# Second cross attention: where the two closing value groups and the output copy of a head stand among the next head's work

## The chip, the cores and the metric

The program runs on one core of one Trainium2 chip. Its engines are TensorE (PE in the profile, PEld for its weight loads), VectorE (DVE), ScalarE (ACT), GpSimd (POOL) and SyncE (SP). The metric is the device time of one execution in microseconds; the time of a kernel is the median over its runs.

## The reference, cut to what matters

The model is a chain of blocks on 256 latent rows of width 256. The block in question is the second cross attention: 16 heads of width 16, 256 queries against 4096 keys.

```python
def _L1_xattn_ref(query, key, value, mask, Wq, bq, Wk, bk, Wv, bv, Wo, bo):
    q = _split_heads(query @ Wq.T + bq)
    k = _split_heads(key @ Wk.T + bk)
    v = _split_heads(value @ Wv.T + bv)
    scores = jnp.einsum('bhqd,bhkd->bhqk', q, k) / jnp.sqrt(jnp.float32(DK))
    scores = jnp.where(mask, scores, jnp.float32(-1000000000.0))
    p = jax.nn.softmax(scores, axis=-1)
    out = jnp.einsum('bhqk,bhkd->bhqd', p, v)
    out = out.transpose(0, 2, 1, 3).reshape(query.shape[0], -1, D)
    return out @ Wo.T + bo
```

The blocks before it (a first cross attention, a self attention, a ternary feed-forward) and behind it (a causal self attention, a mixture of experts) are not touched by the change.

## The kernel before, in words

`stage_cross1` (L1357) holds the block. Every engine has its own instruction stream there, written out by hand; streams meet only at semaphores. The order inside a stream is the order of the text, and nothing plans it.

The 16 heads are walked in pairs (`pairs_of_heads`, L1382): head pair 0 is written out, pairs 1 to 6 are a hardware loop, pair 7 is written out. `b` is the head's place in its pair and picks one of two buffers. One head `h` has these pieces:

- `qk(it, b, g)` (L1568), g = 0 to 7: four TensorE matmuls that write the scores of 512 keys, transposed, into two PSUM banks. Even g use banks 0 and 1, odd g banks 2 and 3. Group 0 waits for `m_rows` of its head, groups wait for the exponential two groups earlier.
- the exponential of group g (L1486) on ScalarE: one ACTIVATE from the two banks into `probs`.
- `pv(h, b, g)` (L1589): the value matmuls of group g, four column blocks of 32, in two passes each (8 matmul records); they add up in PSUM bank 4 over all eight groups. Group 0 waits for `v_staged` and for `acc_copied` of the head before, because it overwrites bank 4.
- `copy_acc(h, b)` (L1500) on ScalarE: copies bank 4 to `acc_sb`, once all eight value groups of head h are done; it raises `acc_copied`.
- `sel(h, b)` (L1600): four small matmuls that read `acc_sb`; VectorE then divides (`normalise`, L1710).
- `m_scores` (L1531): the row maxima of a head are found ahead of time. Sixteen matmuls of 512 keys each per head, taken one head early, rotate over PSUM banks 5 to 7; each is read by one VectorE reduction (L1704), and the bank's next user waits for that read. `m_some(n0, n1)` (L1643) issues the n0-th to (n1-1)-th of them among the current head's work.
- `m_turn` (L1556): two small matmuls at the end of a head that turn the next head's maxima into bank 0; `m_rows` (L1492) on ScalarE then copies them into `q_st`, behind the eighth exponential, and that is what `qk` group 0 of the next head waits for.

TensorE's stream of one head is the `body` at L1637. In short, with the numbers of the groups, before the change:

```text
pv6 pv7 (of the head before) | m0 | qk0 | m1 m2 m3 | qk1 | m4 | qk2 | m5 | pv0 pv1 | m6 | qk3 | m7 m8 m9 | qk4 | m10 |
qk5 | m11 | pv2 pv3 | sel (head before) | m12 | qk6 | m13 | qk7 | m14 m15 | pv4 pv5 | m_turn (next head)
```

Head 0 has no pv6 and pv7 ahead of it and no `sel`. Head 15 has no m's, and head 14 only the first twelve. ScalarE's stream of one head (L1479) is exp0, the copy of the head before, exp1 to exp7, `m_rows` of the next head. POOL stages `v_st` and `q_st` of the next head (L1435), released by the value groups and the scores of the head before the current one; SP loads keys (`load_k1_quarter`, L1348), released by counts of finished score groups (L1416).

Of the kernel before, what the change touches and what calls it, by code (L numbers as in the profile page):

```python
# [1356 lines left out]
def stage_cross1(k):  # L1357
# [18 lines left out]
    def scores_bank(g):  # L1376
        return k.ps[:, 2 * (g % 2):2 * (g % 2) + 2, :].rearrange("p b (c q) -> p (b c) q", q=S)

    def turned(n):
        return k.ps[0:STACK, n, :].bitcast(BF16)  # L1380
# [22 lines left out]
    with nc.Block() as block:  # L1403
# [64 lines left out]
        @block.scalar  # L1468
        def _(act):
            sc = nc.scalar  # L1470
            act.wait_ge(s["q_turned"], 1)
            sc.activation(k.q_st[0:STACK, :, :].rearrange("p b q -> p (b q)"), turned(ACC_BANK)[:, 0:2 * S], ACT.Copy).then_inc(s["q_first"], 1)
            for n in range(H // 4):
                h0 = 2 if n == 0 else 4 * n
                act.wait_ge(s["q_turned"], n + 2)
                sc.activation(k.q_all[0:STACK, h0:4 * n + 4, :].rearrange("p h q -> p (h q)"), turned(n)[:, (h0 - 4 * n) * S:4 * S], ACT.Copy
                              ).then_inc(s["q_stack"], 1)

            def body(it, first, last):  # L1479
                for b in range(2):  # L1480
                    for g in range(groups):
                        n = 16 * it + 8 * b + g
                        act.wait_ge(s["scores"], n + 1)
                        if not (first and b == 0):
                            act.wait_ge(s["pv"], n - groups + 1)
                        sc.activation(probs[:, g], scores_bank(g), ACT.Exp).then_inc(s["exp"], 1)  # L1486
                        if g == 0 and not (first and b == 0):
                            copy_acc(2 * it + b - 1, 1 - b)
                    if not (last and b == 1):
                        m_rows(2 * it + b + 1, 1 - b, first and b == 0)  # L1490

            def m_rows(h, b, fresh=False):  # L1492
                act.wait_ge(s["m_turned"], h + 1)
                if fresh:
                    act.wait_ge(s["q_first"], 1)
                else:
                    act.wait_ge(s["q_staged"], h - 1)
                sc.activation(k.q_st[MAXROW:LOROW, b, :], k.ps[MAXROW:LOROW, 0, 0:S], ACT.Copy).then_inc(s["m_rows"], 1)

            def copy_acc(h, b):  # L1500
                act.wait_ge(s["pv"], groups * h + groups)
                sc.activation(k.acc_sb[:, b, :], k.ps[:, ACC_BANK, 0:S], ACT.Copy).then_inc(s["acc_copied"], 1)

            m_rows(0, 0, True)
            pairs_of_heads(act, body)
            copy_acc(H - 1, 1)

        @block.tensor
        def _(pe):
# [58 lines left out]
            def qk(it, b, g, masked, first):  # L1568
                h, j = 2 * it + b, 2 * b + g // GROUPS
                n = groups * h + g  # L1570
                if g == 0:
                    pe.wait_ge(s["m_rows"], h + 1)
                if g % 2 == 0:
                    pe.wait_ge(k_in[b][g // 2], 16 * K_LOADS1 * (it + 1))
                if not (first and b == 0 and g < 2):
                    pe.wait_ge(s["exp"], n - 1)
                out = scores_bank(g)
                for c in range(GROUP_CH):
                    ch = GROUP_CH * (g % GROUPS) + c
                    last = t.matmul(out[:, c, :], k.k_st[0:STACK, j, ch * P:(ch + 1) * P], k.q_st[0:STACK, b, :],  # L1580
                                    start=True, stop=not masked)
                    if masked:
                        ch = GROUP_CH * g + c
                        for q in range(QT):
                            last = t.matmul(out[:, c, q * P:(q + 1) * P], k.mask_bias[:, q, ch * P:(ch + 1) * P],
                                            k.ident_bf[:, :], start=False, stop=(q == QT - 1))
                last.then_inc(s["scores"], 1)
# [22 lines left out]
            def all_heads(masked):  # L1610
                keep_busy(k, 4, 6, D)
                pe.wait_ge(k.sem("c_aq"), 1)
                o = k.ps[:, 2, :].bitcast(BF16)
                for q in range(QT):
                    for c in range(KT):
                        last = t.transpose(o[:, c * S + q * P:c * S + (q + 1) * P], k.a_q[:, q, c * P:(c + 1) * P], k.ident_bf[:, :])
                last.then_inc(k.sem("c_aqT_ps"), 1)
                pe.wait_ge(k.sem("c_aqT"), 1)
                rows_linear(k, k.a_qT, KT, k.w_tern, None, 3, k.sem("c_y"))
                keep_busy(k, 5, 6)  # L1620
                pe.wait_ge(k.sem("c_xn"), QT)
                transpose_rows(k, k.xn, 2, k.sem("c_xnT_ps"))
                pe.wait_ge(k.sem("c_xnT"), 1)
                rows_linear(k, k.xnT, KT, k.w1_q, None, 3, k.sem("d_q"))
                keep_busy(k, 2, 6)
                pe.wait_ge(s["rows"], 1)
                turn_first()
                for idx in range(n_m):
                    m_scores(0, 0, idx, masked, True, True)
                    if 11 <= idx < 11 + H // 4:  # L1630
                        turn(idx - 11)
                for idx in range(M_AHEAD):
                    m_scores(0, 1, idx, masked, True, True)
                pe.wait_ge(s["q_stack"], H // 4)
                m_turn(0, 0, True)

                def body(it, first, last):  # L1637
                    for b in range(2):
                        h = 2 * it + b
                        behind = not (first and b == 0)  # L1640
                        before = behind and not (first and b == 1)

                        def m_some(n0, n1):  # L1643
                            for x in m_beside(it, b, n0, n1, last):
                                m_scores(*x, masked, first)

                        if behind:
                            pv(h - 1, 1 - b, groups - 2, not before)
                            pv(h - 1, 1 - b, groups - 1, not before)
                        m_some(0, 1)  # L1650
                        qk(it, b, 0, masked, first)
                        m_some(1, 4)
                        qk(it, b, 1, masked, first)
                        m_some(4, 5)
                        qk(it, b, 2, masked, first)
                        m_some(5, 6)
                        pv(h, b, 0, not behind)
                        pv(h, b, 1, not behind)
                        m_some(6, 7)
                        qk(it, b, 3, masked, first)  # L1660
                        m_some(7, 10)
                        qk(it, b, 4, masked, first)
                        m_some(10, 11)
                        qk(it, b, 5, masked, first)
                        m_some(11, 12)
                        pv(h, b, 2, not behind)
                        pv(h, b, 3, not behind)
                        if behind:
                            if last and b == 1:
                                sel(h - 1, 1 - b, n_m * H, H - 2)  # L1670
                            else:
                                sel(h - 1, 1 - b, n_m * (h + 1) + n_m - 2, None)
                        m_some(12, 13)
                        qk(it, b, 6, masked, first)
                        m_some(13, 14)
                        qk(it, b, 7, masked, first)
                        m_some(14, 16)
                        pv(h, b, 4, not behind)
                        pv(h, b, 5, not behind)
                        if not (last and b == 1):  # L1680
                            m_turn(*((it, 1) if b == 0 else (it + 1, 0)))

                pairs_of_heads(pe, body)
                for g in range(groups - 2, groups):
                    pv(H - 1, 1, g, False)
                keep_busy(k, 1, 2, D)
                sel(H - 1, 1, n_m * H, H - 1)
                keep_busy(k, 1, 2, D)

            masked = pe.value_load(k.masked_i[0:1, 0:1], min_val=0, max_val=1)  # L1690
# [503 lines left out]
```

## Time and profile before

| what | value |
|---|---|
| median of 3 runs | 700.41 us (699.09 to 701.73) |
| the profiled execution's own time | 700.59 us |
| its span, first to last instruction | 698.8 us |
| second cross attention, from the first qk to the last copy | about 358.6 to 547.1 us of the span |
| PE, whole span | busy 618.0 us (88%), 5014 matmuls |
| ACT, whole span | busy 453.5 us (65%) |
| DVE, whole span | busy 407.2 us (58%) |

A row of the timeline gives the start in microseconds from the span's start, the time from the first start to the last end of the instructions merged in it, engine, line, operation, output and inputs, shapes, and their number; brackets hold the idle time of that engine before the row and what ended it ("issue" means nothing that the profile shows). Matmuls are pipelined: a matmul's record lasts longer than the step to the next one, so the cost of a piece on TensorE is read from start to start. Times per head are compared from a point of one head to the same point of the next.

### The profile page before, as it was taken

Reading aid. Unit: us, or ns where it says so; the run is one execution under the profiler, and the core shown is the slowest. Engines: PE = TensorE matmul, PEld = TensorE weight load, DVE = VectorE, ACT = ScalarE, POOL = GpSimd, SP = SyncE. Lnnn points to the kernel's source line nnn. Section 1 sums busy time; section 2 is a strip of 40 time slices with the busy share of each in tenths; the row PEclk is TensorE's granted clock in tenths of the full one; section 3 lists DMA queues with packets and bytes.
Section 4 is the critical chain, followed back from the end, with each engine's and each line's share of the span. In section 5 each row is a group of like instructions: output and inputs, shape, how many; then the busy total and the mean of one; then the engine's idle time right before and its main releaser. Section 6 shows DMA issues by size and latency. Waiting matters only on the chain. (4 is left out here: it accounts for less than half of the span.)

```text
span 698.8 us, 14299 instructions
## 1 busy us (share of the span) xinstructions
PE 618.0 (88%) x5014; PEld 374.2 (54%) x5014; DVE 407.2 (58%) x899; ACT 453.5 (65%) x543; POOL 69.1 (10%) x151
## 2 busy tenths in 40 slices
PE   6888887887887888796799999999999998898998
PEld 5554444444344444464345555555554575674886
DVE  6467354222313225876798989898884326645634
ACT  2988999999999993682057767676777215503111
POOL 3001110000010000101211121211110000000000
PEclk8899999999999999998889999999999999999999
DMA  5886786376444113200027633322220570000000
GB/s 132 234 254 206 237 237 211 102 232 173 132 131 127 58 46 118 52 1 3 1 74 248 182 93 81 84 77 86 75 86 10 168 239 1 2 0 1 0 1 15
DMA packets 52904, 73.57 MB, mean 105 GB/s; under 512 B 11044, under 2 KB 29796, under 8 KB 52860
## 3 DMA queue, kind: packets, MB, share of 16 engines
q1 hardware_dynamic: 52091, 72.25, 35.0%
q10 hardware_dynamic: 768, 0.73, 0.4%
q8 instruction: 29, 0.48, 0.3%
q14 instruction: 16, 0.12, 0.1%
HBM read 58.90 MB, written 12.85 MB: 103 GB/s over the span
## 5 line engine op out<-in xcount | busy, mean ns | idle before, releaser
L1704 DVE TENSOR_REDUCE sb_m_blk<-ps 128x1 f32<-128x512 f32 x256 | 159.5, 684 | 18.5 <-PE ps L1550 17.2
L1486 ACT ACTIVATE sb_probs<-ps 128x1024 f32<-128x1024 f32 x128 | 125.8, 1025 | 49.9 <-PE ps L1580 49.3
L656 ACT ACTIVATE sb_probs<-ps 128x1024 f32<-128x1024 f32 x128 | 124.0, 1023 | 10.4 <-PE ps L721 8.9
L661 ACT ACTIVATE sb_probs<-sb_probs,sb_neg_cap,sb_cap 128x4096 f32<-128x4096 f32 (+2 forms) x34 | 121.9, 3591 | 0.1
L740 PE MATMUL ps<-sb_probs,sb_v_st 128*32 128x256 f32 x1024 | 74.5, 388 | 37.2 <-ACT sb_probs L661 37.2
L721 PE MATMUL ps<-sb_q_st,sb_k_st 112*128 112x256 bf16 x512 | 79.3, 280 | 5.2 <-DMA sb_k_st<-k_parts_l 4.4
L1580 PE MATMUL ps<-sb_q_st,sb_k_st 115*128 115x256 bf16 x512 | 76.3, 272 | 1.4 <-ACT sb_probs L1486 1.4
L1550 PE MATMUL ps<-sb_k_st,sb_q_m 96*128 96x512 bf16 x224 | 76.5, 383 | 0.0
L721 PEld LDWEIGHTS ps<-sb_q_st,sb_k_st 112*128 112x128 bf16 x512 | 42.9, 99 | 58.3 <-issue 28.9
L1596 PE MATMUL ps<-sb_probs,sb_v_st 128*32 128x256 f32 x1024 | 67.4, 384 | 0.2 <-ACT sb_probs L1486 0.2
L740 PEld LDWEIGHTS ps<-sb_probs,sb_v_st 128*32 128x32 f32 x1024 | 23.7, 108 | 64.8 <-ACT sb_probs L661 45.5
L1580 PEld LDWEIGHTS ps<-sb_q_st,sb_k_st 115*128 115x128 bf16 x512 | 48.7, 97 | 18.0 <-issue 1.4
L1596 PEld LDWEIGHTS ps<-sb_probs,sb_v_st 128*32 128x32 f32 x1024 | 31.2, 109 | 27.3 <-issue 14.3
L1149 ACT ACTIVATE sb_q_all<-ps,sb_nmax 128x256 f32<-128x256 f32 (+1 forms) x72 | 31.7, 452 | 12.1 <-DVE sb_nmax L1165 12.1
L1018 PE MATMUL ps<-sb_w_o,sb_ones_sq 128*128 128x512 f32 (+1 forms) x82 | 35.0, 564 | 4.8 <-issue 4.8
L1550 PEld LDWEIGHTS ps<-sb_k_st,sb_q_m 96*128 96x128 bf16 x224 | 22.7, 101 | 30.0 <-DVE sb_m_blk L1704 17.1
L617 POOL TENSOR_TENSOR sb_v_st<-sb_v_rows,sb_keep 128x512 f32<-128x512 f32 x14 | 15.9, 1133 | 200.9 <-PE ps L740 161.1
L921 DVE COPY sb_acc_sb<-ps 128x256 f32<-128x256 f32 x16 | 6.8, 424 | 42.3 <-PE ps L740 42.3
L927 DVE RECIPROCAL sb_rec<-ps 128x2 f32<-128x2 f32 x16 | 2.7, 170 | 48.9 <-PE ps L748 48.9
L1165 DVE TENSOR_REDUCE sb_nmax<-ps 128x2 f32<-128x512 f32 (+1 forms) x36 | 22.6, 632 | 13.3 <-PE ps L1088 7.0
L1140 ACT ACTIVATE sb_q_all<-ps 128x512 f32<-128x512 f32 (+1 forms) x36 | 19.8, 551 | 15.6 <-PE ps L1101 15.4
L2008 ACT ACTIVATE sb_probs<-ps 128x512 f32<-128x512 f32 x9 | 5.4, 597 | 36.9 <-PE ps L1966 36.9
(284 smaller groups left out, 846.6 us busy)
## 6 DMA issues: line engine op xcount, KB each, us to landing
sb_k_st<-k_parts_l SPq DMA_DIRECT2D x223, 64.0 KB, 2.0
sb_k_st<-k_parts_l SPq DMA_DIRECT2D x93, 128.0 KB, 3.2
k_parts_l<-sb_v_proj SPq DMA_DIRECT2D x24, 256.0 KB
k_parts_l<-sb_early SPq DMA_DIRECT2D x48, 128.0 KB
sb_v_proj<-ctxT_blocks SPq DMA_DIRECT2D x8, 512.0 KB, 7.0
sb_v_rows<-ctx_by_pair SPq DMA_DIRECT2D x7, 512.0 KB, 4.2
sb_early<-ctxT SPq DMA_DIRECT2D x6, 512.0 KB, 3.8
sb_k_st<-k_parts_l SPq DMA_DIRECT2D x64, 32.0 KB, 1.8
```

The costliest lines, as they stand in the source:

```text
L656: a.activation(probs[:, slot, 4 * g:4 * g + 4, :], scores_bank(g), ACT.Tanh).then_inc(s["tanh"], 1)
L661: a.activation(part, part, ACT.Exp, bias=k.neg_cap[:, 0:1], scale=k.cap[:, 0:1]).then_inc(s["exp"], 1)
L721: last = t.matmul(out[:, c, :], k.k_st[0:STACK0, j, n * P:(n + 1) * P], k.q_st[0:STACK0, j // 2, :], start=True, stop=True)
L740: last = t.matmul(k.ps[32 * m:32 * m + 32, 4 + b, 0:S], k.v_st[:, b, (j % 2) * UNIT_CH + ch, :], probs[:, j % 2, ch, :], start=(j % 2 == 0 ...
L1018: k.nc.tensor.matmul(k.ps[:, bank, 0:cols], k.ones_sq[:, :], k.w1_o[:, :, :].rearrange("p t n -> p (t n)")[:, 0:cols], start=True, stop=True)
L1149: sc.activation(k.sp_rows[:, n % 2, e, 0:nk], a.scores(n)[:, e, 0:nk], ACT.Exp, bias=k.nmax[:, 2 * n + e:2 * n + e + 1], accum_out=k.sums[ ...
L1165: v.tensor_reduce(k.nmax[:, 2 * n:2 * n + 2], a.scores(n)[:, :, 0:nk], AX.X, ALU.max, negate=True).then_inc(s["max"], 1)
L1486: sc.activation(probs[:, g], scores_bank(g), ACT.Exp).then_inc(s["exp"], 1)
L1550: last = t.matmul(o, qs[0:MAXROW, b, q * P:(q + 1) * P], k.k_st[0:MAXROW, 2 * b + blk // (m_blocks // 2), key0:key0 + 512], start=True, st ...
L1580: last = t.matmul(out[:, c, :], k.k_st[0:STACK, j, ch * P:(ch + 1) * P], k.q_st[0:STACK, b, :], start=True, stop=not masked)
L1596: last = t.matmul(k.ps[32 * m:32 * m + 32, ACC_BANK, 0:S], k.v_st[:, b, GROUP_CH * g + m, :], probs[:, g, m, :], start=(g == 0), stop=(g = ...
L1704: v.tensor_reduce(k.m_blk[:, b, q, blk:blk + 1], k.ps[:, m_bank(m_turn_of(idx)), :], AX.X, ALU.max).then_inc(s["m_read"], 1)
```

## The change

On TensorE, the last two value groups of the head before (pv6, pv7) move from the front of a head to behind its score group 0; two of the m matmuls stand ahead of that group and one behind it. On ScalarE, the copy of the head before moves from behind exp0 to behind exp1. No instruction is added or taken away.

```diff
@@ ScalarE, body @@
                         sc.activation(probs[:, g], scores_bank(g), ACT.Exp).then_inc(s["exp"], 1)
-                        if g == 0 and not (first and b == 0):
+                        if g == 1 and not (first and b == 0):
                             copy_acc(2 * it + b - 1, 1 - b)
@@ TensorE, body @@
+                        m_some(0, 2)
+                        qk(it, b, 0, masked, first)
+                        m_some(2, 3)
                         if behind:
                             pv(h - 1, 1 - b, groups - 2, not before)
                             pv(h - 1, 1 - b, groups - 1, not before)
-                        m_some(0, 1)
-                        qk(it, b, 0, masked, first)
-                        m_some(1, 4)
+                        m_some(3, 4)
                         qk(it, b, 1, masked, first)
                         m_some(4, 5)
                         qk(it, b, 2, masked, first)
```

## Rows read from the trace of the kernel before

**Rows 1.** Busy time by engine; columns: stretch, length, PE, PEld, DVE, ACT, POOL, clock, DMA.

```profile
417.62:429.53 11.91, 11.91 (x119) 6.80 (x118) 10.45 (x19) 8.41 (x10) 1.81 (x6) 1.00 0.32 82
...
100.00:111.90 11.90, 10.38 (x101) 6.24 (x94) 5.56 (x9) 11.75 (x10) 1.40 (x2) 1.00 0.66 218
```

**Rows 2.** Waits from 370 to 524.8 us: who, released by, total us, times, longest.

```profile
ACT sb_probs L1486 <- PE ps L1580: 41.6, 48, 1.3
...
PEld ps L1596 <- ACT sb_probs L1486: 2.5, 12, 0.2
```

**Rows 3.** Timeline of PE, the start of one head up to behind its first value groups.

```profile
417.62 0.39 PE L1550 MATMUL ps<-sb_k_st,sb_q_m 96*128 96x512 bf16 x1
417.85 0.60 PE L1580 MATMUL ps<-sb_q_st,sb_k_st 115*128 115x256 bf16 x4
418.29 0.90 PE L1550 MATMUL ps<-sb_k_st,sb_q_m 96*128 96x512 bf16 x3
419.03 0.60 PE L1580 MATMUL ps<-sb_q_st,sb_k_st 115*128 115x256 bf16 x4
...
420.12 0.38 PE L1550 MATMUL ps<-sb_k_st,sb_q_m 96*128 96x512 bf16 x1
420.43 1.07 PE L1596 MATMUL ps<-sb_probs,sb_v_st 128*32 128x256 f32 x16
421.44 0.39 PE L1550 MATMUL ps<-sb_k_st,sb_q_m 96*128 96x512 bf16 x1
```

**Rows 4.** Timeline of PE across the boundary to the next head.

```profile
427.56 1.28 PE L1596 MATMUL ps<-sb_probs,sb_v_st 128*32 128x256 f32 x19
428.46 0.28 PE L1564 MATMUL ps<-sb_ident_bf,sb_m_parts 128*3 128x128 bf16 x2
428.58 1.03 PE L1596 MATMUL ps<-sb_probs,sb_v_st 128*32 128x256 f32 x13
429.54 0.39 PE L1550 MATMUL ps<-sb_k_st,sb_q_m 96*128 96x512 bf16 x1
```

**Rows 5.** Timeline of ACT in the same head and across the same boundary.

```profile
418.49 1.02 ACT L1486 ACTIVATE sb_probs<-ps 128x1024 f32<-128x1024 f32 x1 [1.25 <-PE ps L1580]
419.41 0.38 ACT L1502 ACTIVATE sb_acc_sb<-ps 128x256 f32<-128x256 f32 x1
419.67 1.95 ACT L1486 ACTIVATE sb_probs<-ps 128x1024 f32<-128x1024 f32 x2
...
428.86 0.38 ACT L1498 ACTIVATE sb_q_st<-ps 3x256 bf16<-3x256 f32 x1 [0.34 <-PE ps L1564]
```

**Rows 6.** Timeline of DVE, the last four maxima reads ahead of that boundary.

```profile
426.38 2.48 DVE L1704 TENSOR_REDUCE sb_m_blk<-ps 128x1 f32<-128x512 f32 x4
```

**Rows 7.** Timeline of PEld, the weight loads in the head of rows 3.

```profile
418.18 0.21 PEld L1550 LDWEIGHTS ps<-sb_k_st,sb_q_m 96*128 96x128 bf16 x2
418.80 0.10 PEld L1550 LDWEIGHTS ps<-sb_k_st,sb_q_m 96*128 96x128 bf16 x1 [0.41 <-DVE sb_m_blk L1704]
...
420.43 0.16 PEld L1596 LDWEIGHTS ps<-sb_probs,sb_v_st 128*32 128x32 f32 x8 [0.29 <-issue]
...
421.43 0.10 PEld L1550 LDWEIGHTS ps<-sb_k_st,sb_q_m 96*128 96x128 bf16 x1 [0.41 <-DVE sb_m_blk L1704]
```

**Rows 8.** Timeline of PE in the last head, which has no maxima.

```profile
537.99 0.60 PE L1580 MATMUL ps<-sb_q_st,sb_k_st 115*128 115x256 bf16 x4 [0.77 <-ACT sb_probs L1486]
538.51 1.21 PE L1596 MATMUL ps<-sb_probs,sb_v_st 128*32 128x256 f32 x16
539.65 1.05 PE L1580 MATMUL ps<-sb_q_st,sb_k_st 115*128 115x256 bf16 x8
...
546.02 0.64 PE L1596 MATMUL ps<-sb_probs,sb_v_st 128*32 128x256 f32 x8 [0.16 <-ACT sb_probs L1486]
```

**Rows 9.** Timeline of ACT in the last head.

```profile
535.57 0.38 ACT L1498 ACTIVATE sb_q_st<-ps 3x256 bf16<-3x256 f32 x1
536.82 1.02 ACT L1486 ACTIVATE sb_probs<-ps 128x1024 f32<-128x1024 f32 x1 [0.87 <-PE ps L1580]
...
544.03 1.94 ACT L1486 ACTIVATE sb_probs<-ps 128x1024 f32<-128x1024 f32 x2 [0.87 <-PE ps L1580]
```

## The prediction, made before the result was known

> **What bounds the kernel now.** I read the busy times of stretches first. In one whole head of the second cross attention, 11.91 us long, TensorE's records cover all 11.91 us, VectorE's 10.45 and ScalarE's 8.41 [rows 1]. So the stage runs at TensorE's pace, with VectorE not far behind and ScalarE with room. The table of waits comes second, for the 13 heads from 370 to 524.8 us: ScalarE waits 41.6 us in all for scores, while the value groups' weight loads wait 2.5 us for exponentials, 0.2 us a head [rows 2]. ScalarE waits for TensorE, hardly the other way round. Third come the timelines, from which every step is priced from start to start. Score group 0 starts at 417.85 and the m behind it at 418.29: a score group takes 0.44. The m at 417.62 is followed at 417.85: an m takes 0.22 to 0.23, and I take 0.22 [rows 3].
>
> The change adds no work. It matters only through the order of TensorE's stream and through what each piece waits for there.
>
> **Part 1: the four closing value groups are split into two pairs.** Before, pv4, pv5, m_turn, pv6 and pv7 are one block; after, they are two blocks with m0, m1, qk0 and m2 between them. A lone pair: the m at 420.12 is done at 420.34, the pair starts at 420.43, 0.09 later, and the next m starts at 421.44, 1.01 after the pair [rows 3]. That is 1.10 with both switches. The joined block takes 0.09 and 429.54 - 427.56 = 1.98, together 2.07, and m_turn has 428.58 - 428.46 = 0.12 of it [rows 4]. Two lone pairs and m_turn are 2.20 + 0.12 = 2.32. The split costs 0.25 a head, all of it on TensorE, which nothing covers. Rounding leaves 0.22 to 0.27.
>
> The reason shows in the weight loads. Inside the scores they run ahead: the load at 418.18 belongs to the matmul at 418.29. At a switch they don't: the loads at 420.43 and 421.43 start within 0.01 of their matmuls [rows 7, 3]. The Trainium skill (TensorE: Matmul & The Clock Gate, section "Step-by-step: what each phase is for") says that TensorE pulls weight loads ahead of matmuls in flight when row groups don't conflict or the background weight buffer is the target, so that the next load runs beside the present matmul. By that rule a switch would cost nothing and this term would be 0; the trace agrees within the scores and disagrees at this switch, and I go by the trace.
>
> **Part 2: score group 0 comes before the maxima are ready.** It needs `m_rows`, which ScalarE does behind m_turn, from 428.86 to 429.24 [rows 5]. Before, TensorE spent that time on pv6 and pv7. Now only m0 and m1 stand in between. The pair that starts at 427.56 ends, with m_turn, at 427.56 + 1.01 + 0.12 = 428.69; m0 and m1 take it to 429.13. m1's bank needs the last of four reads, which ends at 426.38 + 2.48 = 428.86 [rows 6], 0.05 ahead of m1's start at 428.91, so at most a few hundredths are lost there. From ScalarE's end to TensorE's start I have two rows: 0.05 (exponential ends at 544.03 + 1.94 = 545.97, value group at 546.02) and 0.15 (exponential ends at 536.82 + 1.02 = 537.84, score group at 537.99) [rows 8, 9]. Between them I take 0.10: qk0 starts at 429.34 and TensorE stands for 0.21. Bounds are 0.16 and 0.26, and up to 0.30 with m1's bank. Queued behind it are m2, the two value groups and so all the rest of the head.
>
> **Part 3: the copy behind exp1.** pv0 of a head overwrites bank 4 and waits for the copy of the head before. exp1 starts 0.64 after qk1's first matmul (419.03 to 419.67). An instruction queued behind an exponential starts 0.92 after it (418.49 to 419.41), the copy takes 0.38 [rows 3, 5], and the release to a value group takes 0.05 as above. So the copy lets pv0 go 0.64 + 0.92 + 0.38 + 0.05 = 1.99 after qk1 starts. TensorE needs 420.43 - 419.03 = 1.40 for qk1, m4, qk2 and m5 [rows 3]. The difference, 0.59, is a new stall in every head; behind it stand pv1, m6 and qk3. I put 0.54 to 0.64 around it. Before, the copy ended at 419.79 [rows 5], 0.64 ahead of pv0, so it cost nothing. ScalarE gives nothing back: pv7 ends well before exp1 can begin, so the copy would have had its place in the idle time there.
>
> **Part 4: what is saved.** m3 waited for VectorE: the three m's at 418.29 and the following qk1 at 419.03 are 0.74 apart instead of 0.66, and the third's load is released by a read [rows 3, 7]. With 1.3 us of qk0's and the value groups' stay ahead of it, that 0.07 goes. qk0 itself and so exp0 come earlier: exp0 at 429.34 + 0.64 = 429.98 instead of 418.49 + 11.91 = 430.40. That is worth nothing, since exp1 now waits for qk1 behind the value pair.
>
> **Other queues.** POOL's staging of `v_st` moves back with pv7, but a head early; SP's key loads follow the score counts, qk0 earlier and qk1 later, and their readers come later by more. Both at nothing; if that cover went, a load's wait would stand before an m.
>
> **The sum.** 0.25 + 0.21 + 0.59 - 0.07 = 0.98 a head, for heads 1 to 14: 13.7 us. Head 15 has no maxima; there `m_rows` ends at 535.95 [rows 9], qk0 would start at 536.05, qk1 at 536.05 + 0.44 + 1.10 = 537.59, and pv0 at 537.59 + 1.99 = 539.58 instead of 538.51. qk3 follows 1.01 later, at 540.59 instead of 539.65 [rows 8]: 0.94. Together 14.6 us. On the span of 698.8 that is 713.4, on the profiled execution's own 700.59 it is 715.2. The median shown, 700.41, stands 0.18 lower, so I say 715.0. With each term at its ends, a head grows by 0.84 to 1.14 us and the kernel lands between 713 and 717.5.
>
> **Rivals.** 0.5% of this kernel is 3.5 us, about what a measurement can tell from no change.
> First, the copy is not late. Should the copy slip in before TensorE has got through qk1 to m5, term 3 falls away, wholly or in part. It decides at 1.99 against 1.40 us. For it: ScalarE has 3.5 us of room in a head [rows 1]. Against it: the copy can't start before exp1, and exp1 can't before qk1's end, so the room is of no use. Wholly gone, 0.39 x 14 = 5.5: 705.9; half gone, 711.
> Second, the switch is free, because the loads are pulled ahead at the new place: 15 x 0.25 = 3.75 less, 711.3. Against it are the three switches of a head that all show their gap. Both together would leave 0.14 x 14 = 2 us, 702.4, within 0.5%.
> Third, faster: ScalarE sets the pace. If what holds a head is its 1.25 us of idle time before exp0 [rows 5], then starting exp0 0.42 earlier shortens each of 15 heads by that: 6.3 us less, 694.1. It decides where TensorE waits in every head at least 0.42 us for exponentials. The rows have 0.2, on weight loads, under a TensorE that is covered throughout [rows 1, 2].
> A falling clock I leave out of the range: the first cross attention keeps 1.00 with 10.38 of 11.90 us covered [rows 1], and the new head would have about 0.8 of 12.9 idle.
>
> **How the numbers follow.** The forecast (all three costs) gets 0.75, the copy wholly or partly hidden 0.10, the free switch 0.10, both together 0.03, ScalarE's pace 0.02. Slower by over 0.5% is 0.75 + 0.10 + 0.10 = 0.95, within 0.5% 0.03, faster 0.02. The range takes in the forecast's 713 to 717.5, the free switch at 711.3 and the upper part of the hidden copy down to 708; I put the top at 718 for the spread of the runs.
>
> **What would show it.** Right, if in the changed trace a head takes about 12.9 us; if PE shows gaps of some 0.2 before L1580 at group 0, released by `sb_q_st` L1498, and of some 0.6 before L1596 at group 0, released by `sb_acc_sb` L1502; if a head has four blocks of value matmuls instead of three; and if VectorE's wait before the m behind the pair is gone. Wrong, if the head stays below 12.4 us, if the copy ends before TensorE gets to pv0, or if ScalarE's idle time shrinks while TensorE has no new gaps.

## The result, and the profile after

The changed kernel takes 717.15 us in the median of 5 runs (715.21 to 720.07), beside 701.73 for 5 runs of the kernel before. The ratio is 1.0216 (95% interval 1.0183 to 1.0250). On the median of 700.41 that is 15.1 us slower (12.8 to 17.5), where 14.6 were forecast. The span of the profiled execution is 713.5 us, where 713.4 were forecast.

One whole head, by the busy times of engines in a stretch, with the columns of [rows 1]:

```profile
434.15:447.23 13.08, 12.34 (x121) 6.64 (x119) 10.59 (x20) 8.52 (x10) 1.81 (x6) 1.00 0.25 72
```

The head has grown from 11.91 to 13.08 us, and TensorE's records no longer cover it: 0.74 us are empty. VectorE and ScalarE are busy for nearly the same time as in [rows 1]. The clock is at its upper level, 2.4 GHz, in both.

The table of waits of the changed kernel, from 372 to 535 us (who, released by, total, times, longest):

```profile
ACT sb_probs L1486 <- PE ps L1580: 52.0, 61, 1.2
...
PEld ps L1596 <- ACT sb_probs L1486: 13.0, 13, 1.0
...
PE ps L1596 <- ACT sb_acc_sb L1502: 8.3, 13, 0.7
...
PEld ps L1580 <- issue: 2.1, 6, 0.4
...
PEld ps L1580 <- ACT sb_q_st L1498: 1.0, 6, 0.2
```

The waits for `sb_acc_sb` and `sb_q_st` are new: TensorE waits for the output copy, 13 times, and for the copied maxima. The row of `sb_q_st` holds six heads, those inside a pair; for the six at the loop's start the profile names no releaser ("issue"), and that score group 0 waits for the maxima there too is shown only by e3. Weight loads of value groups now wait 13.0 us instead of 2.5 [rows 2], once per head; the row names the exponential, but the row of TensorE itself names the copy. ScalarE's own wait for scores did not shrink, it grew from 41.6 to 52.0 us, over 13 heads each time.

TensorE's timeline across the boundary into a head at the loop's start:

```profile
433.04 1.07 PE L1596 MATMUL ps<-sb_probs,sb_v_st 128*32 128x256 f32 x16
433.95 0.28 PE L1564 MATMUL ps<-sb_ident_bf,sb_m_parts 128*3 128x128 bf16 x2
434.15 0.64 PE L1550 MATMUL ps<-sb_k_st,sb_q_m 96*128 96x512 bf16 x2
434.84 0.61 PE L1580 MATMUL ps<-sb_q_st,sb_k_st 115*128 115x256 bf16 x4
435.29 0.38 PE L1550 MATMUL ps<-sb_k_st,sb_q_m 96*128 96x512 bf16 x1
435.60 1.07 PE L1596 MATMUL ps<-sb_probs,sb_v_st 128*32 128x256 f32 x16
436.61 0.39 PE L1550 MATMUL ps<-sb_k_st,sb_q_m 96*128 96x512 bf16 x1
436.83 0.60 PE L1580 MATMUL ps<-sb_q_st,sb_k_st 115*128 115x256 bf16 x4
...
437.93 0.38 PE L1550 MATMUL ps<-sb_k_st,sb_q_m 96*128 96x512 bf16 x1
438.99 1.07 PE L1596 MATMUL ps<-sb_probs,sb_v_st 128*32 128x256 f32 x16 [0.68 <-ACT sb_acc_sb L1502]
439.99 0.39 PE L1550 MATMUL ps<-sb_k_st,sb_q_m 96*128 96x512 bf16 x1
```

Beside it ScalarE's timeline:

```profile
434.34 0.38 ACT L1498 ACTIVATE sb_q_st<-ps 3x256 bf16<-3x256 f32 x1 [0.34 <-PE ps L1564]
435.57 1.02 ACT L1486 ACTIVATE sb_probs<-ps 128x1024 f32<-128x1024 f32 x1 [0.85 <-PE ps L1580]
437.55 1.02 ACT L1486 ACTIVATE sb_probs<-ps 128x1024 f32<-128x1024 f32 x1 [0.96 <-PE ps L1580]
438.47 0.38 ACT L1502 ACTIVATE sb_acc_sb<-ps 128x256 f32<-128x256 f32 x1
```

Four things can be read here. The value pair at 435.60 is a block of its own: it starts 0.09 after the m ahead of it is through (435.29 + 0.22 = 435.51), and the next m follows 1.01 later. That is one more pair of switches. The two m's start 0.26 apart (434.15 + 0.64 - 0.38 = 434.41) instead of 0.22, since m1 now needs a read that has only just ended. Score group 0 could start at 434.63 and starts at 434.84: 0.21, as the maxima are copied until 434.72. And value group 0 could start at 437.93 + 0.31 = 438.24 and starts at 438.99: 0.75, as the copy ends at 438.85.

The boundary inside a pair of heads is milder. TensorE there, first score group 0, then value group 0, and ScalarE's copy of the maxima:

```profile
447.23 0.66 PE L1550 MATMUL ps<-sb_k_st,sb_q_m 96*128 96x512 bf16 x2
447.76 0.61 PE L1580 MATMUL ps<-sb_q_st,sb_k_st 115*128 115x256 bf16 x4
...
450.85 0.38 PE L1550 MATMUL ps<-sb_k_st,sb_q_m 96*128 96x512 bf16 x1
451.83 1.07 PE L1596 MATMUL ps<-sb_probs,sb_v_st 128*32 128x256 f32 x16 [0.60 <-ACT sb_acc_sb L1502]
```

```profile
447.33 0.38 ACT L1498 ACTIVATE sb_q_st<-ps 3x256 bf16<-3x256 f32 x1 [0.19 <-PE ps L1564]
```

m1 starts at 447.23 + 0.66 - 0.38 = 447.51, and score group 0 at 447.76, where 447.51 + 0.22 = 447.73 was possible: 0.03. The copy of the maxima ends at 447.71. Value group 0 could start at 450.85 + 0.31 = 451.16 and starts at 451.83: 0.67.

### The profile page after: what moved, and what is told of

Its sections match the earlier page's. It is cut to its first block and busy times, and to the rows that moved or that the text cites. A ratio compares the mean times of both kernels' runs of the same rounds, so it can differ in the third digit from the quotient of the medians.

```text
span 713.5 us, 14299 instructions
## 1 busy us (share of the span) xinstructions
PE 621.5 (87%) x5014; PEld 372.0 (52%) x5014; DVE 408.7 (57%) x899; ACT 454.5 (64%) x543; POOL 68.9 (10%) x151
## 5 line engine op out<-in xcount | busy, mean ns | idle before, releaser
L1705 DVE TENSOR_REDUCE sb_m_blk<-ps 128x1 f32<-128x512 f32 x256 | 161.4, 684 | 31.0 <-PE ps L1550 31.0
L1550 PE MATMUL ps<-sb_k_st,sb_q_m 96*128 96x512 bf16 x224 | 78.2, 383 | 0.0
L740 PEld LDWEIGHTS ps<-sb_probs,sb_v_st 128*32 128x32 f32 x1024 | 23.7, 108 | 65.4 <-ACT sb_probs L661 46.3
L1596 PEld LDWEIGHTS ps<-sb_probs,sb_v_st 128*32 128x32 f32 x1024 | 27.9, 109 | 40.8 <-ACT sb_probs L1486 16.1
```

The source lines that it names most:

```text
L740: last = t.matmul(k.ps[32 * m:32 * m + 32, 4 + b, 0:S], k.v_st[:, b, (j % 2) * UNIT_CH + ch, :], probs[:, j % 2, ch, :], start=(j % 2 == 0 ...
L1550: last = t.matmul(o, qs[0:MAXROW, b, q * P:(q + 1) * P], k.k_st[0:MAXROW, 2 * b + blk // (m_blocks // 2), key0:key0 + 512], start=True, st ...
L1596: last = t.matmul(k.ps[32 * m:32 * m + 32, ACC_BANK, 0:S], k.v_st[:, b, GROUP_CH * g + m, :], probs[:, g, m, :], start=(g == 0), stop=(g = ...
L1705: v.tensor_reduce(k.m_blk[:, b, q, blk:blk + 1], k.ps[:, m_bank(m_turn_of(idx)), :], AX.X, ALU.max).then_inc(s["m_read"], 1)
```

## The experiments

Since heads alternate, the measure is a pair of heads: the time from the first exponential of a head to that of the head two later, in the middle of the stage. It repeats within 0.02 us through the loop and does not hang on what happens elsewhere in the program. The stage is taken from the start of the first exponential to the start of the last. The last column sets the times of a kernel's runs against those of the kernel before taken with them.

| kernel | pair of heads, us | against before | stage, us | ratio of times (95%) |
|---|---|---|---|---|
| before | 23.81 | | 185.7 | |
| changed | 25.91 | +2.10 | 200.9 | 1.0216 (1.0183 to 1.0250) |
| e1, copy put back | 24.48 | +0.67 | 190.8 | 1.0069 (1.0046 to 1.0091) |
| e2, copy moved alone | 25.25 | +1.44 | 196.0 | 1.0153 (1.0109 to 1.0198) |
| e3, m_turn earlier | 25.65 | +1.84 | 199.1 | one run |
| e4, one switch more | 24.30 | +0.49 | 190.5 | 1.0057 (1.0027 to 1.0087) |
| e5, both stalls taken away | 24.22 | +0.41 | 188.4 | 1.0059 (1.0029 to 1.0088) |
| e6, one switch less | 25.21 | +1.40 | 196.3 | one run |

The rows behind the pairs of before, changed and e5 are these, of ScalarE's timeline, one fence for each:

```profile
430.48 1.02 ACT L1486 ACTIVATE sb_probs<-ps 128x1024 f32<-128x1024 f32 x1 [1.25 <-PE ps L1580]
...
454.29 1.02 ACT L1486 ACTIVATE sb_probs<-ps 128x1024 f32<-128x1024 f32 x1 [1.25 <-PE ps L1580]
```

```profile
435.57 1.02 ACT L1486 ACTIVATE sb_probs<-ps 128x1024 f32<-128x1024 f32 x1 [0.85 <-PE ps L1580]
...
461.48 1.02 ACT L1486 ACTIVATE sb_probs<-ps 128x1024 f32<-128x1024 f32 x1 [0.85 <-PE ps L1580]
```

```profile
432.33 1.02 ACT L1486 ACTIVATE sb_probs<-ps 128x1024 f32<-128x1024 f32 x1 [0.95 <-PE ps L1580]
...
456.55 1.02 ACT L1486 ACTIVATE sb_probs<-ps 128x1024 f32<-128x1024 f32 x1 [0.95 <-PE ps L1580]
```

Three theories stood against each other. Theory A: three separate costs, the switch, the maxima and the copy. Theory B: the moved value pair costs it all, wherever the copy stands. Theory C: the copy's place costs it all.

### e1: the copy back behind the first exponential

```diff
-                        if g == 1 and not (first and b == 0):
+                        if g == 0 and not (first and b == 0):
                             copy_acc(2 * it + b - 1, 1 - b)
```

> The changed kernel with the copy put back behind the first exponential; the value pair stays behind score group 0. Theory A (three separate costs: switch, maxima, copy): the stall of 0.68 and 0.60 us before value group 0 goes, a pair of heads shrinks from 25.91 to about 24.5 us, the span from 713.5 to about 703 (a half-clock stretch behind the stage can add 1). Theory B (the moved value pair is the whole cost, wherever the copy stands): the span stays at 712 to 714. Theory C (the copy's place is the whole cost): the span is back at 698 to 700.

The pair falls by 1.43 us, and the time is 0.7% above before instead of 2.2%. ScalarE's timeline, then TensorE's, at such a head:

```profile
446.70 0.39 ACT L1502 ACTIVATE sb_acc_sb<-ps 128x256 f32<-128x256 f32 x1 [0.22 <-PE ps L1596]
447.44 1.94 ACT L1486 ACTIVATE sb_probs<-ps 128x1024 f32<-128x1024 f32 x2 [0.35 <-PE ps L1580]
```

```profile
447.89 0.38 PE L1550 MATMUL ps<-sb_k_st,sb_q_m 96*128 96x512 bf16 x1
448.20 1.07 PE L1596 MATMUL ps<-sb_probs,sb_v_st 128*32 128x256 f32 x16
```

The copy takes time in which ScalarE has nothing else to do: ahead of it ScalarE waits 0.22 for the value pair of the head before, behind it 0.35 for the scores of group 1. Value group 0 follows its m by 0.31, the m's own 0.22 and the 0.09 of the switch, with no wait. Theory B falls, and so does C, since 0.67 of the pair is left. The span is 706.4, not 703; the stage accounts for 5.1 of the 7.6 us above before, 1.3 lie ahead of it and 1.2 behind it (last section).

### e2: the copy moved alone

```diff
-                        if g == 0 and not (first and b == 0):
+                        if g == 1 and not (first and b == 0):
                             copy_acc(2 * it + b - 1, 1 - b)
```

> The kernel before with nothing but the copy moved behind the second exponential. Theory A: value group 0 stands 0.6 to 0.75 us for the copy in 15 heads, the span goes from 698.8 to 708 or 709, no other gap. Theory B: at most 1 us more than before, since the copy is then early enough without the value pair in the way. Theory C: about 713.

The copy alone costs 1.44 a pair. That and e1's remainder, 0.67, make 2.11 against the 2.10 of the whole change: the two halves of the edit neither hide nor raise each other. The span is 708.7, as theory A had it; theories B (at most 1 us) and C (about 713) miss it. TensorE at value group 0:

```profile
421.68 0.38 PE L1550 MATMUL ps<-sb_k_st,sb_q_m 96*128 96x512 bf16 x1
422.67 0.64 PE L1596 MATMUL ps<-sb_probs,sb_v_st 128*32 128x256 f32 x8 [0.61 <-ACT sb_acc_sb L1502]
```

### e3: the maxima turned earlier

```diff
                         pv(h, b, 4, not behind)
-                        pv(h, b, 5, not behind)
                         if not (last and b == 1):
                             m_turn(*((it, 1) if b == 0 else (it + 1, 0)))
+                        pv(h, b, 5, not behind)
```

> The changed kernel with the two transposes of the maxima (m_turn) one value group earlier, between value groups 4 and 5. Theory A: ScalarE copies the maxima 0.3 to 0.4 us earlier, score group 0 no longer waits for them, a pair of heads shrinks by about 0.27 us (0.22 in the head at the loop's end, 0.05 in the other) and the span by about 2 us. Rival: score group 0 is held by the bank of the second m or by its keys; then its gap stays and the span is the same within 0.5 us.

The pair falls by 0.26 and the stage by 1.8 us. (The span of this one execution, 717.1, is longer than that of the changed kernel, not 2 us shorter: its stage begins 3.5 us later, and what lies behind the stage takes 1.9 us more.) TensorE, then ScalarE:

```profile
437.06 0.64 PE L1550 MATMUL ps<-sb_k_st,sb_q_m 96*128 96x512 bf16 x2
437.54 0.60 PE L1580 MATMUL ps<-sb_q_st,sb_k_st 115*128 115x256 bf16 x4
```

```profile
436.93 0.38 ACT L1498 ACTIVATE sb_q_st<-ps 3x256 bf16<-3x256 f32 x1
```

The maxima are copied by 436.93 + 0.38 = 437.31, and score group 0 follows m1 (437.06 + 0.64 - 0.38 = 437.32) by 0.22, one m, with no gap. So it was the maxima that held score group 0, not its keys. m1's few hundredths stay: they belong to the bank.

### e4: one switch more

```diff
-                        m_some(5, 6)
                         pv(h, b, 0, not behind)
+                        m_some(5, 6)
                         pv(h, b, 1, not behind)
```

> The kernel before with the sixth m put between value groups 0 and 1, which makes one switch more between value groups and other matmuls in every head and moves no wait. Theory A: 0.23 to 0.26 us more a head, for 14 heads, so 3.2 to 3.7 us: a span of about 702.4. By the rule that weight loads are pulled ahead of matmuls in flight: nothing, 698.8.

The pair grows by 0.49, 0.24 a head. TensorE there:

```profile
425.10 0.64 PE L1596 MATMUL ps<-sb_probs,sb_v_st 128*32 128x256 f32 x8
425.67 0.39 PE L1550 MATMUL ps<-sb_k_st,sb_q_m 96*128 96x512 bf16 x1
425.99 0.64 PE L1596 MATMUL ps<-sb_probs,sb_v_st 128*32 128x256 f32 x8
426.56 0.39 PE L1550 MATMUL ps<-sb_k_st,sb_q_m 96*128 96x512 bf16 x1
```

Two value groups with the m between them take 1.46; the lone pair of [rows 3] took 1.01 and an m 0.22, so the switch costs 0.23 again, here with nothing moved that waits. The span was forecast at 702.4 and is 708.5 in the profiled execution. The stage grew by 4.8 us, of which 3.4 are 14 heads of 0.24. The other 1.4 are the first head, 12.95 us instead of 11.52: the granted clock is 0.50 there from 360.91 to 364.33 us, and 1.00 in the first head of the kernel before. The 10 runs spread from 702.58 to 710.6; the pair, not the total, carries this verdict.

### e5: both stalls taken away

This is e3's edit of m_turn together with e1's edit of the copy:

```diff
                         pv(h, b, 4, not behind)
-                        pv(h, b, 5, not behind)
                         if not (last and b == 1):
                             m_turn(*((it, 1) if b == 0 else (it + 1, 0)))
+                        pv(h, b, 5, not behind)
...
-                        if g == 1 and not (first and b == 0):
+                        if g == 0 and not (first and b == 0):
```

> The changed kernel with both stalls taken away at once: the copy back behind the first exponential and m_turn between value groups 4 and 5. What is left of the change is the split of the value block. Theory A, by adding up what the first runs showed: a pair of heads of 24.49 - 0.26 = 24.2 us against 23.82 before, 0.2 us a head for the switch less what the third m saves, so the stage (first to last exponential) about 189 us against 185.7. If the costs overlapped, so that taking one away bares another, the pair stays at 24.4 or above. If the earlier first exponential were worth something once nothing else stands in the way, the pair falls below 23.8.

24.22 is what the sum gave. What remains, 0.41 a pair or 0.20 a head, is the switch (0.24) and m1's wait (about 0.05) less the 0.07 that m3 saves. The first exponential of a head does come earlier (the first two are 10.78 us apart, before 11.52), and that gives nothing: the kernel is still 0.6% slower than before.

### e6: one switch less

```diff
                         m_some(5, 6)
-                        pv(h, b, 0, not behind)
-                        pv(h, b, 1, not behind)
                         m_some(6, 7)
...
                         m_some(11, 12)
-                        pv(h, b, 2, not behind)
-                        pv(h, b, 3, not behind)
+                        for g in range(4):
+                            pv(h, b, g, not behind)
```

> The kernel before with value groups 0 and 1 moved back to stand directly ahead of 2 and 3: one switch less in every head, and the m's not spread anew. If the switch were all that counts, 0.24 us less a head: a pair of 23.3 us, a stage of about 182. My expectation: slower, because VectorE (10.45 of 11.91 us busy) then gets its m's in bursts and TensorE waits for the banks: m's ahead of the block wait about 0.3 us each, and four value groups in a row leave VectorE idle; a head of about 12.6 us, a stage of about 196.

Fewer switches did not make a faster head: 0.70 more each, a head of 12.6 and a stage of 196.3 us, as expected. TensorE waits for the banks of the m's ahead of the block, and VectorE has nothing to do behind it. TensorE, then VectorE:

```profile
437.22 0.38 PE L1550 MATMUL ps<-sb_k_st,sb_q_m 96*128 96x512 bf16 x1
437.75 0.39 PE L1550 MATMUL ps<-sb_k_st,sb_q_m 96*128 96x512 bf16 x1
...
438.42 0.92 PE L1550 MATMUL ps<-sb_k_st,sb_q_m 96*128 96x512 bf16 x2
439.55 0.39 PE L1550 MATMUL ps<-sb_k_st,sb_q_m 96*128 96x512 bf16 x1 [0.21 <-DVE sb_m_blk L1702]
```

```profile
443.71 0.17 DVE L1711 RECIPROCAL sb_rec<-ps 128x2 f32<-128x2 f32 x1 [1.03 <-PE ps L1606]
```

The m at 437.75 could have followed at 437.22 + 0.22 = 437.44; the third of the m's that begin at 438.42 could have started at 438.42 + 0.44 = 438.86 and starts at 439.55. That is 0.31 + 0.69 = 1.00 of waits against the 0.24 of a switch. VectorE then waits 1.03 us for `sel`, which stands behind the block. So the value pairs before the change, costly as their switches are, are also what spreads the m's for VectorE. An order with a switch less and the m's spread anew was not tried; of those tried, none beats the kernel before.

## Why the prediction was right, step by step

**Part 1, the split: right.** 0.25 a head was forecast, 0.24 is what e4 measures with nothing else moved. The Trainium skill (TensorE: Matmul & The Clock Gate, section "Step-by-step: what each phase is for") has weight loads pulled ahead of matmuls in flight when row groups don't conflict or the background weight buffer is the target. That would have made the term 0 if either held at a switch; the loads of value groups start with their matmuls, and no run shows why neither helps there.

What the value groups have apart from the other matmuls is their type (f32, not bf16) and their tiles (32 columns, not 128). `sel` has the type of the one and the tiles of the other. Its weight loads in the last head of the kernel before, and those of the scores behind it:

```profile
542.92 0.52 PEld L1606 LDWEIGHTS ps<-sb_quad_sum,sb_acc_sb 128*128 128x128 f32 x4 [0.41 <-issue]
543.28 0.87 PEld L1580 LDWEIGHTS ps<-sb_q_st,sb_k_st 115*128 115x128 bf16 x8
```

From the value groups to `sel` the tile changes and the type doesn't: the load starts with its matmul (542.92). From `sel` to the scores the type changes and the tile doesn't: the load starts 0.11 ahead of its matmul (543.39). So these rows put the switch down to the tile; no run changed it alone.

**Part 2, the maxima: right in kind, too large.** 0.21 a head was forecast. It is 0.21 in heads at the loop's start and 0.03 in the others, 0.26 a pair by e3. I read one boundary, and there are two kinds. At the loop's start ScalarE begins the copy of the maxima 0.34 behind its last work, and score group 0 starts 434.84 - 434.72 = 0.12 behind the copy; inside a pair these are 0.19 and 447.76 - 447.71 = 0.05. Why the loop's start is the slower one was not tried. m1's wait for its bank, set at a few hundredths at most and left out of the sum, is 0.04 and 0.06.

**Part 3, the copy: right in kind, too small.** 0.59 a head was forecast, 0.75 and 0.67 came, 1.43 a pair by e1 and 1.44 by e2. The mis-sized terms are two. The release to the value group took 438.99 - 438.85 = 0.14, where 0.05 was taken from a value group that waits for an exponential alone; this one waits for the exponential, the staged values and the copy. And in heads at the loop's start exp1 follows qk1's start by 437.55 - 436.83 = 0.72, not 0.64. Whether it is the several waits that make the release later was not tried.

**Part 4, what is saved: right.** Behind the pair, m3 and qk1 are 436.83 - 436.61 = 0.22 apart, with no wait left. The earlier first exponential is worth nothing, as e5 shows.

**The sum: right partly by luck.** In the loop a head costs 2.10 / 2 = 1.05 more, where 0.98 was forecast. That it is so near has luck in it: part 2 was 0.08 a head too large and part 3 0.12 too small. (The terms at their lower ends give 0.22 + 0.16 + 0.54 - 0.07 = 0.85, not 0.84.) In the last head value group 0 waits too, 1.04 us on TensorE. The stage grew by 15.2 us. The span grew by only 14.65, since the stage begins 0.6 later and what lies behind it took 1.1 us less in this execution (next section but one); so the forecast span of 713.4 is met closer than the mechanism was.

**The rivals.** That the copy slips in early is refuted by the 13 waits of TensorE for the copy, one a head. The free switch is refuted by e4. ScalarE's pace is refuted by e5: the first exponential is earlier and the head longer. The other queues, put at nothing, cost nothing: in the table of waits of the changed kernel no row has TensorE wait for a load or for POOL.

## What to carry to other kernels

Where one engine was covered throughout and another waited for it, starting the waiting engine sooner bought nothing (e5); what counted was what the move does to the covered engine's own stream, each switch and each new wait. Here a copy that frees an accumulator belonged in the first idle time behind the accumulator's end (e1), not behind the next long instruction, which has to wait for the very stream that the copy holds up (e2). Price a moved piece at every kind of boundary that the loop has, not at the one that is read first.

## What the runs showed that was not expected

The part behind the stage is the same work in all kernels, yet it took 152.7 to 156.3 us. Busy times from the last exponential of the stage to the end, in the kernel before, in the changed one and in e4, with the columns of [rows 1]:

```profile
544.95:698.80 153.85, 139.61 (x856) 103.84 (x844) 77.08 (x229) 37.78 (x124) 1.06 (x5) 0.99 0.15 49
```

```profile
560.74:713.40 152.66, 138.21 (x856) 103.05 (x844) 77.08 (x229) 37.72 (x124) 1.05 (x5) 1.00 0.15 49
```

```profile
552.25:708.50 156.25, 142.45 (x856) 105.91 (x844) 77.19 (x229) 37.89 (x124) 1.05 (x5) 0.97 0.15 48
```

VectorE's and ScalarE's work agrees within 0.2 us. TensorE's takes the longer, the lower the mean granted clock is: 138.2 us at 1.00, 139.6 at 0.99, 142.5 at 0.97. One place shows how. The kernel before, then the changed kernel, around the same matmuls of the last block:

```profile
627.60:630.80 3.20, 1.46 (x11) 0.99 (x12) 1.60 (x4) 1.67 (x8) 0.00 (x0) 1.00 0.00 0
630.80:634.20 3.40, 3.40 (x15) 1.85 (x12) 2.37 (x7) 2.04 (x8) 0.00 (x0) 0.50 0.00 0
```

```profile
643.40:646.60 3.20, 1.48 (x12) 0.99 (x12) 1.62 (x4) 1.67 (x8) 0.00 (x0) 1.00 0.00 0
646.60:650.00 3.40, 2.90 (x24) 1.56 (x20) 3.10 (x10) 2.71 (x10) 0.00 (x0) 1.00 0.00 0
```

TensorE was busy for 1.46 and 1.48 of 3.2 us ahead of it; then one execution went to the lower level (0.50 is 1.2 GHz) and the other stayed at the upper. It is the only stretch at the lower level in this part of the one execution, and the other has none: the part takes 153.88 and 152.74 us, so the loss is 1.1 us. The other profiled executions fall in line: one such stretch in e5 (153.9 us), two in e1, e2 and e3 (154.6 to 155.1), three in e4 and e6 (156.3). The work is the same in all of them; why an execution gets more or fewer stays open. Differences of half a percent are therefore better read from a pair of heads at full clock than from totals.
